# Linear attention on 32 by 32 PE tiles: block-diagonal pairs of tokens instead of groups of eight, and a block transpose for kv

## The chip, the cores and the metric

The kernel runs on one core of a Trainium2 chip (trn2). The metric is device time in microseconds (us) from start to end of one execution; the median of three runs is compared.

## What is computed

x is 8 by 512 tokens of 256 features, float32, that is 4096 tokens. Three residual parts follow each other: half of a mixture-of-experts layer (8 experts, 256 slots each), a linear-attention block with an MLP, and half of the experts layer again. The change touches the attention alone, which mixes the 16 heads of one token, never two tokens:

```python
q = (xn @ wq + bq).reshape(b, n, H, HD).transpose(0, 2, 1, 3)   # H = 16 heads of HD = 16; k and v alike
fq = jax.nn.elu(q) + 1.0
fk = jax.nn.elu(k) + 1.0
kv = jnp.einsum('bhnd,bhne->bnde', fk, v)       # per token: 16 x 16, summed over heads
qkv = jnp.einsum('bhnd,bnde->bhne', fq, kv)     # per token and head
k_sum = fk.sum(axis=1)
qk = jnp.einsum('bhnd,bnd->bhn', fq, k_sum)
attn = qkv / (qk[..., None] + 1e-06)
```

## The kernel before

The first experts stage runs to about 163 us, the middle stage (attention and MLP) to about 600 us, the second experts stage to the end. The middle stage takes 32 tiles of 128 tokens in a software pipeline: in step s of `MID_STEPS`, each engine's program does a fixed list of pieces, written out by hand, each for another tile. TensorE (PE) projects q, k and v of tile s-2 (`qkv`), forms kv of tile s-4 (`sum_kv`, L1989) and its product with the queries (`sum_att`, L2006), turns and projects the result of tile s-5 (`turn_o`, `project`), turns tile s-6 for the MLP and, from step 10, adds one group's MLP products (`up_mid`, `down_mid`). Each engine runs its list in order; semaphores join the lists. Before step 10 the PE program has no MLP work and pads itself with idle products.

The attention needs the features with heads or feature numbers on partitions. So `store_grids` (L553) writes q, k and v of a tile to HBM, and they are read back 64 bytes at a time: the tile is cut into 16 sets of eight tokens; `issue_keys` (L370) reads, for one of the eight tokens t of every set, keys onto the 16 partitions t*16 to t*16+15 and columns t*16 to t*16+15, so that `keys` [128 partitions, 16 sets, 128] is block-diagonal (the zeros were put there once by `clear_grids`, L762). `issue_queries` (L377) does the same for the queries, and one transfer brings all values (L567), with a column of ones for k_sum. With the store these are 18 transfers a tile. SyncE's queue (SP) issues them; in the first seven tiles (`HELPED`, L362) ScalarE (ACT) issues some (`help_keys`, `help_queries`, L1005 to L1019).

`sum_kv` then makes, per set, values.T @ keys: 128 partitions into 32 rows by 128 columns, four sets beside each other on the four 32-column tiles of the PE array, all into one PSUM bank (`B_ATT`). Its result is kv transposed, so it goes through ACT (`copy_kvt`, L1021, 128 by 512), four PE transposes (`turn_kv`, L2000) and a VectorE (DVE) copy (L1679) before `sum_att` multiplies it with the queries, 16 products again. `attended` (L1571) turns blocks of 32 by 32 on DVE (L1576) and divides.

Of the kernel before, what the change touches and what calls it, by code (L numbers as in the profile page):

```python
# [27 lines left out]
def build(nc, x_in, ln1_w, ln1_b, wq, bq, wk, bk, wv, bv, wo, bo, ln2_w, ln2_b,  # L28
# [19 lines left out]
    SETS = P // 8  # L48
# [10 lines left out]
    qkv_rows = nc.dram_tensor("qkv_rows", [3, T, D], F32).ap()  # L59

    with ExitStack() as ctx:
# [144 lines left out]
        with ExitStack() as phase:  # L206
            x_all = tile(phase, "x_all", [P, NT, D])
            tile(phase, "below_values", [P, 2, SETS, 32])
# [36 lines left out]
        with ExitStack() as mid:  # L245


            keys = tiles(mid, "keys_", 2, [P, SETS, P])
            queries = tiles(mid, "queries_", 2, [P, SETS, P])
            values = tiles(mid, "values_", 2, [P, SETS, 32])  # L250
            feats = tiles(mid, "feats_", 2, [P, 3 * D])
            kvt = tile(mid, "kvt_", [P, 4, P])
            kv = tile(mid, "kv_", [P, 4, P])
# [58 lines left out]
        s_st1, s_kvt, s_kvturn, s_kv = sem("kv_t_summed"), sem("kv_t_copied"), sem("kv_turned"), sem("kv_copied")  # L312
# [49 lines left out]
        HELPED = 7  # L362

        def keys_by_sp(n):
            return (4 if n == 0 else 5) if n < HELPED else 8

        def queries_by_sp(n):
            return (2 if n == 0 else 6) if n < HELPED else 8

        def issue_keys(engine, n, t):  # L370

            i, rows = n % 2, slice(n * P, (n + 1) * P)
            engine.dma_start(keys[i][t * HEADS:(t + 1) * HEADS, :, t * HD:(t + 1) * HD],  # L373
                             qkv_rows[1, rows, :].rearrange(
                                 "(s t) (h d) -> t h s d", t=8, h=HEADS)[t]).then_inc(s_kvin[i], 16)

        def issue_queries(engine, n, t):  # L377
            i, rows = n % 2, slice(n * P, (n + 1) * P)
            engine.dma_start(queries[i][t * HD:(t + 1) * HD, :, t * HEADS:(t + 1) * HEADS],
                             qkv_rows[0, rows, :].rearrange(  # L380
                                 "(s t) (d h) -> t d s h", t=8, d=HD)[t]).then_inc(s_qin[i], 16)

        def set_of(i, j):

            return 4 * j + i
# [53 lines left out]
        def _(sp):  # L439
# [113 lines left out]
            def store_grids(n):  # L553
                i, rows = n % 2, slice(n * P, (n + 1) * P)
                sp.wait_ge(s_feat, n + 1)
                sp.wait_ge(s_val, n + 1)
                sp.dma_start(qkv_rows[:, rows, :].rearrange("c p d -> p c d"),
                             feats[i][:].rearrange("p (c d) -> p c d", c=3)).then_inc(s_grid[i], 16)

            def load_keys(n):  # L560
                i, rows = n % 2, slice(n * P, (n + 1) * P)
# [5 lines left out]
                sp.dma_start(values[i][:, :, 0:HD], qkv_rows[2, rows, :].rearrange(  # L567
                    "(s t) (g e) -> (t g) s e", t=8, g=HEADS)).then_inc(s_kvin[i], 16)
                for t in range(keys_by_sp(n)):
                    issue_keys(sp, n, t)  # L570

            def load_queries(n):
                if n >= 2:
                    sp.wait_ge(s_st2, n - 1)
                for t in range(queries_by_sp(n)):
                    issue_queries(sp, n, t)
# [270 lines left out]
        def _(act):  # L847
# [146 lines left out]
            def qkv(n):  # L994
                soft = feats[n % 2][:, 0:2 * D]
                act.wait_ge(s_qk, n + 1)
                if n >= 2:
                    act.wait_ge(s_grid[n % 2], 16 * (n // 2))
# [5 lines left out]

            def help_queries(n):  # L1005
                act.wait_ge(s_grid[n % 2], 16 * (n // 2 + 1))
                if n >= 2:
                    act.wait_ge(s_st2, n - 1)
                for t in range(queries_by_sp(n), 8):
                    issue_queries(act, n, t)  # L1010

            def help_keys(n):
                act.wait_ge(s_grid[n % 2], 16 * (n // 2 + 1))
                if n == 0:
                    act.wait_ge(s_zeros, 6)
                if n >= 2:
                    act.wait_ge(s_st1, n - 1)
                for t in range(keys_by_sp(n), 8):
                    issue_keys(act, n, t)  # L1019

            def copy_kvt(n):  # L1021
                act.wait_ge(s_st1, n + 1)
                if n >= 1:
                    act.wait_ge(s_kvturn, n)
                act.copy(kvt[:], bank[B_ATT][:].rearrange("p (i c) -> p i c", i=4)).then_inc(s_kvt, 1)
# [18 lines left out]
            for s in range(MID_STEPS):  # L1044
                if at(s, 2) is not None:
                    turn_zn(s - 2)
                if s == 4:
                    help_queries(0)
                if s == 5:
                    help_keys(2)  # L1050
# [5 lines left out]
                if at(s, 4) is not None and s != 4:  # L1056
                    copy_kvt(s - 4)
# [12 lines left out]
                if 6 <= s < HELPED + 3:  # L1070
                    help_keys(s - 3)
                if at(s, 2) is not None:
                    qkv(s - 2)
                if s == 4:
                    help_keys(1)
                    copy_kvt(0)
                if routed(s, 1) is not None and routed(s, 1) < NG - 2:
                    soften(routed(s, 1))
                if s == 3:
                    help_keys(0)  # L1080
# [4 lines left out]
                if at(s, 3) is not None and 1 <= s - 3 < HELPED:  # L1085
                    help_queries(s - 3)
# [1130 lines left out]
```

## Time and profile before

| | |
|---|---|
| median of 3 runs | 728.15 us (726.8 to 728.37) |
| span of the profiled execution, first to last instruction | 726.3 us |
| PE busy | 670.9 us (92%), 6214 matmul instructions |
| DVE, ACT, POOL busy | 481.1, 420.1, 326.5 us |
| hardware DMA queue q1 (SP's) | 272298 packets, 48.9% of 16 engines' span |
| HBM traffic | 130 GB/s over the span |

The profiled execution's own time is its span and some 1.85 us around it, by the median of the runs. Busy shares are averages over stages, and matmuls overlap, so a busy PE says nothing about how well it is used. PEld is the load of the stationary operand, which is an instruction of its own. A float32 matmul of the program appears as two matmuls and two loads in the profile (called passes below); a float32r product is three matmuls of one pass each.

### The profile page before, as it was taken

To read this page: it belongs to the slowest core of one execution; us is meant where nothing else is said; L and a number is where in the kernel's file an instruction comes from. 1 tells how busy PE (TensorE), PEld (TensorE's weight loads), DVE (VectorE), ACT (ScalarE), POOL (GpSimd) and SP (SyncE) were. 2 spreads that over 40 slices of the span, in tenths; PEclk is the share of its full clock that TensorE was granted. 3 is DMA by queue.
4 is the path that set the end of the run, shared out by engine and by line. 5 is a ranking of instruction groups with operands and counts; after the bars stand their busy time and mean duration, and the time that the engine had idled before them with its cause. 6 is when DMAs were issued, how large, how long until landed. Compare 5 with 4: busy or idle time off the path is not lost.

```text
span 726.3 us, 17454 instructions
## 1 busy us (share of the span) xinstructions
PE 670.9 (92%) x6214; PEld 567.6 (78%) x6214; DVE 481.1 (66%) x1332; ACT 420.1 (58%) x841; POOL 326.5 (45%) x493
## 2 busy tenths in 40 slices
PE   7689999998777999999999999999999885999994
PEld 5449999975566788888888888888888663999994
DVE  7856757425688766767777768677676565777751
ACT  5755556502334767676767676766754642766660
POOL 5234563122232453545573664745547563353312
PEclk9879999999999999999999999999999998999998
DMA  8479788404656444544555555555433343567720
GB/s 264 149 241 322 229 270 276 139 29 119 98 99 109 91 66 90 95 87 66 101 86 85 117 84 129 68 108 91 86 73 96 116 132 109 167 215 217 219 93 29
DMA packets 287104, 95.56 MB, mean 132 GB/s; under 512 B 213989, under 2 KB 284737, under 8 KB 287019
## 3 DMA queue, kind: packets, MB, share of 16 engines
q1 hardware_dynamic: 272298, 85.48, 48.9%
q0 software_dynamic: 3840, 8.32, 3.6%
q10 hardware_dynamic: 10880, 0.66, 1.0%
q8 instruction: 50, 0.82, 0.5%
q14 instruction: 36, 0.29, 0.1%
HBM read 65.09 MB, written 29.40 MB: 130 GB/s over the span
## 4 chain that ended last, share of the span: by engine, by line
PE 75%; DVE 8%; issue 6%; ACT 4%; POOL 2%; DMA 2%; SPq 1%; ACTq 1%; POOLq 0%; DVEq 0%
PE bank L1735 68%; PE bank L1744 7%; DMA qkv_rows<-feats 1%; POOL hids L795 1%; SPq L373 1%; ACTq L373 1%; ACT hids L1038 1%; DMA x_all<-in_L_attn_q_x_dram 1%; ACT feats L1001 1%; POOL table L677 1%; ACT feats L999 0%; DVE kv_ L1679 0%; ACT ots L1063 0%; DVE sth L1687 0%; DVE att_ L1576 0%
## 5 line engine op out<-in xcount | busy, mean ns | idle before, releaser
L1735 PE MATMUL bank<-down_w,hids 128*128 128x256 f32 x768 | 105.8, 286 | 1.9 <-POOL hids L795 1.6
L1735 PE MATMUL bank<-hnts,up_w 128*128 128x512 f32 x384 | 104.4, 407 | 0.0
L795 POOL TENSOR_TENSOR hids<-hid,hids 128x512 fp32r<-128x512 f32 x64 | 83.1, 1298 | 41.0 <-ACT hids L1038 40.6
L1735 PEld LDWEIGHTS bank<-down_w,hids 128*128 128x128 f32 x768 | 95.7, 188 | 6.2 <-POOL hids L795 3.4
L1735 PE MATMUL bank<-qkv_w,xnts 128*128 128x256 f32 (+1 forms) x384 | 76.4, 346 | 5.7 <-DVE xnts L1589 4.8
L1735 PEld LDWEIGHTS bank<-hnts,up_w 128*128 128x128 f32 x384 | 67.5, 189 | 11.4
L1735 PEld LDWEIGHTS bank<-qkv_w,xnts 128*128 128x128 f32 x384 | 60.6, 189 | 18.2 <-DVE xnts L1589 7.5
L1035 ACT ACTIVATE hid<-bank,cols 128x512 f32<-128x512 f32 x64 | 44.1, 688 | 45.8 <-PE bank L1735 45.5
L786 POOL TENSOR_SCALAR sth<-sth 128x1 f32<-128x1 f32 x32 | 7.2, 226 | 125.3 <-DVE sth L1601 125.3
L1735 PE MATMUL bank<-a_w,xa_h 128*128 128x256 f32 x256 | 60.2, 379 | 0.0
L1735 PE MATMUL bank<-xa_xt,a_w 128*128 128x256 f32 x384 | 55.1, 294 | 1.4 <-DVE xa_xt L1327 1.4
L1735 PE MATMUL bank<-xb_xt,b_w 128*128 128x256 f32 x384 | 52.9, 287 | 1.4 <-DVE xb_xt L1327 1.4
L1735 PEld LDWEIGHTS bank<-xa_xt,a_w 128*128 128x128 f32 x384 | 49.0, 189 | 3.1 <-DVE xa_xt L1327 1.6
L900 ACT ACTIVATE xa_h<-bank,cols 128x256 f32<-128x256 f32 x64 | 26.8, 470 | 40.8 <-PE bank L1735 40.8
L1735 PEld LDWEIGHTS bank<-a_w,xa_h 128*128 128x128 f32 x256 | 46.3, 190 | 5.1
L1735 PEld LDWEIGHTS bank<-xb_xt,b_w 128*128 128x128 f32 x384 | 48.5, 188 | 2.4 <-DVE xb_xt L1327 1.6
L900 ACT ACTIVATE xb_h<-bank,cols 128x256 f32<-128x256 f32 x64 | 26.9, 471 | 35.0 <-PE bank L1735 35.0
L1569 DVE TENSOR_TENSOR ots<-bank,ots 128x256 fp32r<-128x256 f32 x32 | 13.5, 423 | 50.4 <-ACT ots L1063 50.4
L984 ACT CAST xnts<-bank 128x256 fp32r<-128x256 f32 x32 | 12.0, 374 | 59.9 <-PE bank L1744 57.5
L1038 ACT ACTIVATE hids<-bank,cols 128x512 fp32r<-128x512 f32 x64 | 43.6, 681 | 0.0
L1290 DVE TENSOR_TENSOR b_w<-b_raw,b_w 128x512 fp32r<-128x512 f32 x32 | 23.9, 748 | 22.4 <-ACT b_w L876 22.1
L711 POOL DMA_INDIRECT out_dram<-xb_fin,xb_slot x16 | 17.1, 1067 | 48.2 <-DVE xb_fin L1350 46.1
(272 smaller groups left out, 1546.9 us busy)
## 6 DMA issues: line engine op xcount, KB each, us to landing
qkv_rows<-feats SPq DMA_DIRECT2D x32, 384.0 KB, 3.4
a_raw<-in_L_ffn_w_dram SPq DMA_DIRECT2D x32, 256.0 KB, 4.1
a_w<-in_L_ffn_w_dram SPq DMA_DIRECT2D x32, 256.0 KB, 3.7
b_raw<-in_L_ffn_w_dram SPq DMA_DIRECT2D x32, 256.0 KB, 3.2
b_w<-in_L_ffn_w_dram SPq DMA_DIRECT2D x32, 256.0 KB, 3.0
mid_rows<-x_all SPq DMA_DIRECT2D x8, 512.0 KB, 2.9
x<-mid_rows SPq DMA_DIRECT2D x32, 128.0 KB, 2.4
values<-qkv_rows SPq DMA_DIRECT2D x32, 128.0 KB, 2.9
```

What stands on the lines that cost most here:

```text
L373: engine.dma_start(keys[i][t * HEADS:(t + 1) * HEADS, :, t * HD:(t + 1) * HD], qkv_rows[1, rows, :].rearrange("(s t) (h d) -> t h s d", t= ...
L677: pool.indirect_dma_start(table, bass.IndirectOffsetOnAxis(ap=dest_b[g % 2][:, i:i + 1], axis=0), entry_b[g % 2][:, i], None, bounds_check ...
L711: pool.indirect_dma_start(ex.target, bass.IndirectOffsetOnAxis(ap=ex.buf.slot[:, c - ex.first * ST], axis=0), ex.buf.fin[c % 4][:], None, ...
L795: pool.tensor_tensor(hids[1][u % 3][:], hid[u % 2][:], f32(hids[0][u % 3][:]), ALU.subtract).then_inc(s_hidl, 1)
L900: act.activation(ex.buf.h[u % 4][:, i], dst[:, i * CAP:(i + 1) * CAP], ACT.Relu, bias=bias).then_inc(ex.sem.relu, 1)
L984: act.copy(xnts[0][n % 2][:], bank[B_TURN][:, 0:D].rearrange("p (k t) -> p k t", k=KD)).then_inc(s_xnh, 1)
L1035: act.activation(hid[u % 2][:], bank[b][:], ACT.Gelu, bias=bias).then_inc(s_hid, 1)
L1038: act.activation(hids[0][u % 3][:], bank[b][:], ACT.Gelu, bias=bias).then_inc(s_hid, 1)
L1290: dve.tensor_tensor(low[cut], ex.raw[cut], f32(high[cut]), ALU.subtract).then_inc(ex.sem.low1, 1)
L1569: dve.tensor_tensor(ots[1][n % 2][:], bank[B_KV][:, 0:D], f32(ots[0][n % 2][:]), ALU.subtract).then_inc(s_ol, 1)
L1735: return pe.matmul(dst, left, right, start=start, stop=stop, skip_group_check=True)
L1744: return pe.matmul(dst, src, ident[:], is_transpose=True, start=start, stop=stop, skip_group_check=True)
```

## The change

The tile is cut otherwise: four bands of 32 tokens (`BANDS`), each of 16 pairs (`PAIR_TOKENS`). A pair's keys lie block-diagonally in 32 partitions (two tokens by 16 heads) by 32 columns, so `keys`, `queries`, `values` and `kv` are all [128, 16, 32], with band c on partitions 32c to 32c+31. Every product of `sum_kv` and `sum_att` is now 32 partitions by 32 by 32, on the diagonal tile (c, c) of the PE array, and there are 64 of each per tile. kv is read from PSUM by one DVE block transpose; ACT's copy, the four PE transposes and the DVE copy are gone. Two transfers each bring keys, values and queries (one per token of a pair, on every second partition), and the store is four transfers, one per band: ten in all, issued by SP alone. Two dummy tiles keep the addresses of what lies behind the now smaller ones.

```diff
-    SETS = P // 8
+    PAIR_TOKENS, BANDS = 2, 4
+    SETS = P // (PAIR_TOKENS * BANDS)
...
+    qkv_rows = nc.dram_tensor("qkv_rows", [3, T // BANDS, BANDS * D], F32).ap()
...
+        def band_rows(i, n):
+            return qkv_rows[i, n * P // BANDS:(n + 1) * P // BANDS, :]
+
+        def of_token(grid, t):
+
+            return grid[t::PAIR_TOKENS]
+
+        def store_band(engine, n, c):
+            i, q = n % 2, P // BANDS
+            engine.dma_start(qkv_rows[:, n * q:(n + 1) * q, c * D:(c + 1) * D].rearrange("i q d -> q i d"),
+                             feats[i][c * q:(c + 1) * q, :].rearrange("p (i d) -> p i d", i=3)).then_inc(s_grid[i], 16)
 
         def issue_keys(engine, n, t):
+            i = n % 2
+            engine.dma_start(of_token(keys[i], t)[:, :, t * HD:(t + 1) * HD],
+                             band_rows(1, n).rearrange("(s t) (g d) -> t g s d", t=PAIR_TOKENS, d=HD)[t]).then_inc(
+                s_kvin[i], 16)
...
             def load_keys(n):
-                sp.wait_ge(s_grid[i], 16 * (n // 2 + 1))
+                sp.wait_ge(s_grid[n % 2], 16 * BANDS * (n // 2 + 1))
...
-                for t in range(keys_by_sp(n)):
+                for t in range(PAIR_TOKENS):
                     issue_keys(sp, n, t)
+                for t in range(PAIR_TOKENS):
+                    issue_values(sp, n, t)
...
                 if n4 is not None:
-                    dve.wait_ge(s_kvturn, n4 + 1)
+                    dve.wait_ge(s_st1, n4 + 1)
                     if n4 >= 1:
                         dve.wait_ge(s_st2, n4)
-                    dve.tensor_copy(kv[:], bank[B_KV][:].rearrange("p (i c) -> p i c", i=4)).then_inc(s_kv, 1)
+                    dve.transpose(kv[:], bank[B_ATT][:].rearrange("p (s t d) -> p s d t", s=SETS, t=PAIR_TOKENS)).then_inc(s_kv, 1)
...
-                for i in range(4):
-                    for j in range(4):
-                        last = mm(bank[B_ATT][32 * j:32 * j + 32, i * P:(i + 1) * P], values[n % 2][:, set_of(i, j)],
-                                  keys[n % 2][:, set_of(i, j)], True, True)
+                for g in range(SETS):
+                    for c in range(BANDS):
+                        band = slice(32 * c, 32 * c + 32)
+                        last = mm(bank[B_ATT][band, 32 * g:32 * g + 32], values[n % 2][band, g], keys[n % 2][band, g], True, True)
                 last.then_inc(s_st1, 1)
```

`sum_att` changes as `sum_kv` does; `help_keys`, `help_queries`, `copy_kvt` and `turn_kv` are taken out with their calls.

How the instructions stand on PE in one step with the MLP, before (`hnts`, `down_w` are the MLP's, `zn_`, `on`, `kvt_`, `hn_` are operands that are turned):

```order
L1735 MATMUL bank<-hnts_0,up_w 128x512 x6
L1735 MATMUL bank<-keys,values 32x128 x16
L1744 MATMUL bank<-ident,on 128x128 x2
L1735 MATMUL bank<-qkv_w,xnts_0 128x512 x6
L1735 MATMUL bank<-qkv_w,xnts_0 128x256 x6
L1735 MATMUL bank<-down_w,hids_0 128x256 x12
L1744 MATMUL bank<-ident,kvt_ 128x128 x4
L1735 MATMUL bank<-o_w,ots_1 128x256 x6
L1744 MATMUL bank<-ident,hn_ 128x128 x2
L1735 MATMUL bank<-hnts_0,up_w 128x512 x6
L1735 MATMUL bank<-queries,kv_ 32x128 x16
```

and with the change:

```order
L1702 MATMUL bank<-hnts_0,up_w 128x512 x6
L1702 MATMUL bank<-keys,values 32x32 x64
L1711 MATMUL bank<-ident,on 128x128 x2
L1702 MATMUL bank<-qkv_w,xnts_0 128x512 x6
L1702 MATMUL bank<-qkv_w,xnts_0 128x256 x6
L1702 MATMUL bank<-down_w,hids_0 128x256 x12
L1702 MATMUL bank<-o_w,ots_1 128x256 x6
L1711 MATMUL bank<-ident,hn_ 128x128 x2
L1702 MATMUL bank<-hnts_0,up_w 128x512 x6
L1702 MATMUL bank<-queries,kv_ 32x32 x64
```

The 16 products with 128 columns become 64 with 32, twice, and the four transposes of `kvt_` between `down_w` and `o_w` are gone; nothing else on PE moves.

ACT in such a step, between the MLP's gelus and the copy of v (L1003) before:

```order
L1038 ACTIVATE hids_1<-bank,cols 128x512
L1025 COPY kvt_<-bank 128x512
L1063 CAST ots_1<-bank 128x256
L1069 ACT_TABLE_LOAD
L1069 ACTIVATE scrap<-minus_half 128x1
L999 ACTIVATE feats<-bank 128x512
L1001 ACTIVATE feats<-feats 128x512
L1003 COPY feats<-bank 128x256
```

and with the change:

```order
L1020 ACTIVATE hids_2<-bank,cols 128x512
L1039 CAST ots_0<-bank 128x256
L1045 ACT_TABLE_LOAD
L1045 ACTIVATE scrap<-minus_half 128x1
L1003 ACTIVATE feats<-bank 128x512
L1005 ACTIVATE feats<-feats 128x512
L1007 COPY feats<-bank 128x256
```

The copy to `kvt_` ahead of the cast of `ots` is gone; the rest keeps its order.

SP over one step, before:

```order
L373 DMA keys<-qkv_rows 16x16x16 x8
L549 DMA x_4<-mid_rows 128x256
L557 DMA qkv_rows<-feats 128x3x256
L379 DMA queries<-qkv_rows 16x16x16 x8
L567 DMA values<-qkv_rows 128x16x16
L373 DMA keys<-qkv_rows 16x16x16 x8
```

and with the change:

```order
L383 DMA values<-qkv_rows 64x16x16 x2
L555 DMA x_4<-mid_rows 128x256
L372 DMA qkv_rows<-feats 32x3x256 x4
L389 DMA queries<-qkv_rows 64x16x16 x2
L377 DMA keys<-qkv_rows 64x16x16 x2
L383 DMA values<-qkv_rows 64x16x16 x2
```

The store becomes four issues and the reads six, each of 1024 pieces of 64 bytes where the old ones had 256 (values 2048); their order in the step stays: store, queries, keys and values.

## Rows read from the trace of the kernel before

**Rows 1.** Busy time by stretch: us, PE, PEld, DVE, ACT, POOL, clock, DMA share, GB/s.
```profile
190.00:230.00 40.00, 31.01 (x387) 23.54 (x385) 31.42 (x76) 14.95 (x37) 12.42 (x30) 1.00 0.62 96
...
350.00:430.00 80.00, 79.79 (x881) 68.10 (x880) 59.90 (x162) 55.27 (x101) 50.02 (x82) 1.00 0.57 97
```
**Rows 2.** Timeline, PE: start, us, instruction; from `turn_o` to the transposes of one step.
```profile
247.42 0.44 PE L1744 MATMUL bank<-ident,on 128*128 128x128 f32 x2
...
251.23 0.60 PE L1744 MATMUL bank<-ident,kvt_ 128*128 128x128 f32 x4
```
**Rows 3.** One tile's rows: `keys` passes of PE: ns min/median/max, first and last start.
```profile
L1735 PE MATMUL bank<-keys,values x1024: 269/273/297, 181.7 to 541.3; 128*32 128x128 f32 x171
```
**Rows 4.** Timeline, ACT, the same stretch as rows 2.
```profile
247.68 0.59 ACT L1025 COPY kvt_<-bank 128x512 f32<-128x512 f32 x1
248.14 0.40 ACT L1063 CAST ots<-bank 128x256 fp32r<-128x256 f32 x1
...
251.11 0.35 ACT L1003 COPY feats<-bank 128x256 f32<-128x256 f32 x1
```
**Rows 5.** Timeline, loads for `o_w` behind the transposes, one step early, one late.
```profile
251.56 0.78 PEld L1735 LDWEIGHTS bank<-o_w,ots 128*128 128x128 f32 x6
...
410.82 0.35 ACT L1003 COPY feats<-bank 128x256 f32<-128x256 f32 x1
...
411.49 0.78 PEld L1735 LDWEIGHTS bank<-o_w,ots 128*128 128x128 f32 x6
```
**Rows 6.** Timeline, PE, one `sum_att`: cut at 401.71, at 401.86, and whole.
```profile
401.69 0.32 PE L1735 MATMUL bank<-queries,kv_ 128*32 128x128 f32 x4
...
401.69 0.43 PE L1735 MATMUL bank<-queries,kv_ 128*32 128x128 f32 x8
...
401.69 1.08 PE L1735 MATMUL bank<-queries,kv_ 128*32 128x128 f32 x32
```
**Rows 7.** PE on one tile: float32 passes of 256 columns, bfloat16 ones of 24.
```profile
L1735 PE MATMUL bank<-a_w,xa_h 128*128 128x256 f32 x256 | 60.2, 379 | 0.0
...
102.12 1.89 PE L1735 MATMUL bank<-a_w,xa_h 128*128 128x256 f32 x8
...
L1735 PE MATMUL bank<-rb_left_factor,rb_mark x16: 187/188/209, 604.5 to 607.9; 128*128 128x24 bf16 x16
...
604.48 0.37 PE L1735 MATMUL bank<-rb_left_factor,rb_mark 128*128 128x24 bf16 x8
```
**Rows 8.** Groups of load instructions: count, busy us, mean ns, idle before.
```profile
L1735 PEld LDWEIGHTS bank<-hnts,up_w 128*128 128x128 f32 x384 | 67.5, 189 | 11.4
...
L1735 PEld LDWEIGHTS bank<-queries,kv_ 128*32 128x32 f32 x1024 | 26.0, 109 | 11.1 <-issue 9.1 <-DVE kv_ L1679 2.0
```
**Rows 9.** Busy time of `keys` instructions, 0.1 us after a wait: PE, PEld, clock.
```profile
196.46:196.56 0.10, 0.07 (x4) 0.10 (x8) 0.00 (x0) 1.00 0.14 15
```
**Rows 10.** Timeline, ACT, early steps; last, a piece of the chain that ended last.
```profile
190.99 0.59 ACT L1025 COPY kvt_<-bank 128x512 f32<-128x512 f32 x1 [3.31 <-issue]
...
225.81 2.44 ACTq L373 DMA_DIRECT2D keys<-qkv_rows  x2
228.35 0.60 ACT L999 ACTIVATE feats<-bank 128x512 f32<-128x512 f32 x1 [2.46 <-PE bank L1735]
...
235.78 0.59 ACT kvt_ L1025
```
**Rows 11.** SP's issues: ns min/median/max; one step's keys; us from issue to landing.
```profile
L373 SPq DMA_DIRECT2D keys<-qkv_rows x234: 303/449/2612, 176.1 to 533.8; - x117
...
245.17 5.50 SPq L373 DMA_DIRECT2D keys<-qkv_rows  x8
...
qkv_rows<-feats SPq DMA_DIRECT2D x32, 384.0 KB, 3.4
```
**Rows 12.** DVE's two operations over 128x512: ns min/median/max.
```profile
L1679 DVE COPY kv_<-bank x32: 678/691/693, 185.1 to 544.9; 128x512 f32<-128x512 f32 x32
...
L1576 DVE STREAM_TRANSPOSE att_<-bank x32: 701/704/716, 187.0 to 548.3; 128x512 f32<-128x512 f32 x32
```

More of the change, by code:

```diff
@@ L245, in build @@
         with ExitStack() as mid:
-            keys = tiles(mid, "keys_", 2, [P, SETS, P])
-            queries = tiles(mid, "queries_", 2, [P, SETS, P])
+            keys = tiles(mid, "keys_", 2, [P, SETS, 32])
+            queries = tiles(mid, "queries_", 2, [P, SETS, 32])
             values = tiles(mid, "values_", 2, [P, SETS, 32])
+            tile(mid, "weights_come_early", [P, 6 * KD * D * 2])
             feats = tiles(mid, "feats_", 2, [P, 3 * D])
-            kvt = tile(mid, "kvt_", [P, 4, P])
-            kv = tile(mid, "kv_", [P, 4, P])
+            kv = tile(mid, "kv_", [P, SETS, 32])
+            tile(mid, "weights_come_early_too", [P, KD * D])
             att = tile(mid, "att_", [P, HEADS, 32])
@@ L359, in build, with issue_values @@
         LAST_SENT = PASSED_IN_STEPS - GROUP
[L362 to L368, printed above, removed]
-        def issue_keys(engine, n, t):
[L372 to L375, printed above, removed]
-        def issue_queries(engine, n, t):
[L378 to L385, printed above, removed]
+        def band_rows(i, n):
[6 more added lines that the diff above has]
+                             feats[i][c * q:(c + 1) * q, :].rearrange("p (i d) -> p i d", i=3)).then_inc(s_grid[i], 16)
+        def issue_keys(engine, n, t):
+            i = n % 2
+            engine.dma_start(of_token(keys[i], t)[:, :, t * HD:(t + 1) * HD],
+                             band_rows(1, n).rearrange("(s t) (g d) -> t g s d", t=PAIR_TOKENS, d=HD)[t]).then_inc(
+                s_kvin[i], 16)
+        def issue_values(engine, n, t):
+            i = n % 2
+            engine.dma_start(of_token(values[i], t)[:, :, 0:HD],
+                             band_rows(2, n).rearrange("(s t) (g e) -> t g s e", t=PAIR_TOKENS, e=HD)[t]).then_inc(
+                s_kvin[i], 16)
+        def issue_queries(engine, n, t):
+            i = n % 2
+            engine.dma_start(of_token(queries[i], t)[:, :, t * HEADS:(t + 1) * HEADS],
+                             band_rows(0, n).rearrange("(s t) (g h) -> t g s h", t=PAIR_TOKENS, h=HEADS)[t]).then_inc(
+                s_qin[i], 16)
         pieces = [
@@ L574, in load_queries @@
                     sp.wait_ge(s_st2, n - 1)
-                for t in range(queries_by_sp(n)):
+                for t in range(PAIR_TOKENS):
                     issue_queries(sp, n, t)
@@ L1003, in qkv @@
                 act.copy(feats[n % 2][:, 2 * D:3 * D], bank[B_V][:, 0:D]).then_inc(s_val, 1)
[L1005 to L1025, printed above, removed]
             def gelus(g, m):
@@ L1046, in _ @@
                     turn_zn(s - 2)
[L1047 to L1050, printed above, removed]
                 g_up, j_up = divmod(s - 10, GROUP)
@@ L1084, in _ @@
                     turn_h(s - 6)
-                if at(s, 3) is not None and 1 <= s - 3 < HELPED:
-                    help_queries(s - 3)
                 if 0 <= g_up < NG:
@@ L1575, in attended @@
                 dve.wait_ge(s_st2, n + 1)
-                dve.transpose(att[:], bank[B_ATT][:].rearrange("p (i t h) -> p h i t", i=4, t=8)).then_inc(s_att, 1)
+                dve.transpose(att[:], bank[B_ATT][:].rearrange("p (s t h) -> p h s t", s=SETS, t=PAIR_TOKENS)).then_inc(s_att, 1)
                 dve.wait_ge(s_att, step + 1)
@@ L2120, in _ @@
                     down_mid(g_down, 2 * j_down + 1)
-                if at(s, 4) is not None:
-                    if kv_free:
-                        pe.wait_ge(*kv_free)
-                    turn_kv(s - 4)
-                    kv_free = (s_kv, s - 3)
                 for n in turned_at(s, 0):
```

43 lines of the change are left out of this document (12 added, 31 removed).

## The prediction, made before the changed kernel was run

> **What bounds the kernel now.** I read the busy time by stretch first. From 350 to 430 us PE is busy 79.8 of 80 us at a granted clock of 1.00 (2.4 GHz), DVE 59.9, ACT 55.3 [rows 1]: with the MLP in the step nothing but PE sets the pace. From 190 to 230 us, before the MLP's products start, PE is busy 31.0 of 40 and DVE 31.4 [rows 1]; there a loop of PE, ACT and DVE sets the step. The page of the profile has SP's queue on the 16 DMA engines for half the span, but a PE that is busy all the time waits for no transfer. So the transfers, which the change is said to be about, can pay only before some 240 us; behind that the change is worth what it does to PE. `sum_kv` runs from 181.7 to 541.3 us [rows 3]; the one of tile 7 ends at 247.4 us, where `turn_o` starts [rows 2], so 25 tiles (7 to 31) stand under the PE bound, some 12.3 us each ((541.3 - 246.4)/24).
>
> **PE, what goes.** The four transposes of `kvt_`: four passes in 0.60 us, the last of which lasts 0.27 by itself, so 0.33/3 = 0.11 us apart [rows 2], 0.43 us a tile. (A pass's length is taken from its siblings of 128 columns, 273 ns [rows 3].)
>
> **PE, what is dearer.** A `sum_att` is 32 passes in 1.08 us. The timeline cut short shows how: the first four last 0.32 us together and 0.297 each, so they start some 7 ns apart, one on each 32-column tile; with the next four it is 0.43. Every 0.11 us four passes start side by side, eight times: 0.87 us [rows 3, 6]. Now there are 128 passes, 32 on each tile. What one takes is not in the trace, since no pass has 32 columns on 32 partitions; so I bound it.
> - From below: float32 passes of 256 columns start (1.89 - 0.38)/7 = 0.216 us apart [rows 7], those of 128 columns 0.109: 0.84 ns a column, so 30 ns for 32. The load of 128 columns takes 189 ns, that of 32 109 [rows 8]: 0.83 ns a column, 27 ns for 32, if the rest is a latency that overlaps. It does overlap on one tile: bfloat16 products start (0.37 - 0.19)/7 = 26 ns apart [rows 7]. And four starts 7 ns apart need 28 ns. All three give 30 ns a round, 32 x 30 = 0.96 us.
> - From above: a round costs what it costs now, 0.109 us, 32 x 0.109 = 3.5 us.
>
> I take 0.96, since it is the rows of the same kind (float32, four tiles beside each other) carried down in columns. That PE's sequencer can deliver is shown right behind a wait: within 0.1 us from 196.46 on, eight loads of `sum_kv` had started [rows 9]. In program order load and pass alternate, so the eighth load is the 15th instruction: 7 ns each at most. 256 instructions in 0.96 us want 3.8 ns each, which no row shows for so long; this is the weakest step. So +0.1 us for `sum_kv` and +0.1 for `sum_att`.
>
> Before, every product used all 128 rows of the array, and four column tiles wrote one PSUM bank side by side [rows 6]; now four row tiles write the bank `B_ATT`, each its own 32 partitions. The rule that speaks against it is in the Trainium skill, TensorEngine Tiling (Array Packing), Gotcha 1: PSUM Pressure: different row tiles cannot use one PSUM bank at the same time. No row here shows such a case; by the rule the sum would be that of the third rival below.
>
> **What stands behind the transposes.** PE's next piece, `project`, waits for ACT's copy of v. In the early step this copy ends at 251.11 + 0.35 = 251.46 us and the loads for `o_w` start at 251.56; in the late one at 411.17 and 411.49 [rows 4, 5]. So where the gap is 0.10, ACT must come earlier for PE to gain. It does: the copy to `kvt_` goes, which sits 0.46 us ahead of the cast of `ots`. But the cast waits for `turn_o`, whose end, 247.42 + 0.44 = 247.86, moves to 247.96; the cast then starts at about 248.00 in place of 248.14 [rows 2, 4], and all behind it 0.14 earlier. I count half of the gap of 0.10 as the signal's own time. So such a step gains 0.05 + 0.14 = 0.19 in its first half, and 0.09 with the 0.1 of `sum_att` off. In the late step the slack is 0.27 + 0.14, more than PE's 0.43 - 0.10 = 0.33, so it keeps 0.33, less 0.1: 0.23. I take 4 tiles of the early kind (until the turned rows of the second router come between, from step 15 on) and 21 of the late: 0.4 + 4.8 = **5.2 us less**.
>
> **DVE.** The block transpose takes the place of the copy at the same point of its list, 704 ns for 691 [rows 12]: +0.01 a tile. It now waits for `sum_kv` itself, long done. Nothing.
>
> **DMA.** SP issues 18 and a row of x now, up to 5.5 us for eight keys [rows 11]; afterwards 10, at the median 0.45 each 4.5 us. The pieces of 64 bytes are as many as before (6144 a tile). In the first steps the store's four issues push its landing 3 x 0.45 = 1.4 us back, and 3.4 us of landing are no longer covered by eight issues of queries; in return keys and values take four issues for nine, 2.3 us less, on SP alone. That is about even. ACT, however, stops helping: at 190.99 it comes to its copy after 3.31 us in which the profile shows it waiting for nothing, while its queue issued keys; at 225.81 two issues take 2.44 us, and the features start right behind them at 228.35, for which I put 0.5, an estimate; and the `kvt_` copy of 0.59 us at 235.78 is on the chain that ended last [rows 10], 0.46 in its queue. I take 1.0 + 0.5 + 0.4 = 1.9 us less. Bounds: 0 (the transfers' chain replaces it) and 4 (three issues behind one another on SP no longer stand in the way). Five steps in which the loop over DVE binds have `sum_att` in it: +0.5. Together **1.4 less**.
>
> **The sum.** 726.3 - 5.2 - 1.4 = 719.7 us of span. The median of the runs lies 1.85 us over this span: **721.5 us**. A round of 35 ns in place of 30 would add 2 x 0.16 x 30 = 10 us at most, so the forecast hangs on a few ns; with 30 ns and the DMA bounds it is 719 to 723.5, with 28 to 33 ns 717 to 728.
>
> **The rivals.**
> - **Gain eaten up.** Rounds of 32 to 34 ns, or a start that waits for four stores: 726 to 730 us; centre 728. For it: 28 ns of starts and 30 of columns leave no reserve. Chance 0.13.
> - **Load and pass take turns on a tile** (27 + 30 = 57 ns a round). `sum_kv` and `sum_att` take 1.82 us, +0.95 each. PE: 25 x (1.9 - 0.43) = +37 us, first steps +6: 771 us. It decides from about 34 ns a round on. For it: in all stages with four tiles the load ended just when the older pass had run out (109 and 109 ns), so the trace doesn't show them overlapping there; against it, one tile with 24 columns does. Chance 0.15. This is the rival on the other side.
> - **The bands take turns at the bank**, as the rule has it: 128 x 30 ns = 3.8 us, +2.97 twice; 25 x (5.9 - 0.43) = +137, first steps some +20: 885 us. For it: no row has several row tiles. Against: they write different partitions, and four column tiles share the bank now. Chance 0.08.
> - **Starts stay 26 ns apart**, as on one tile [rows 7], at either level of the clock: 128 x 26 = 3.3 us, +2.46 twice; 25 x 4.5 + 16 = +129: 857 us. Against it, four starts 7 ns apart [rows 6], but never more than four in a row. The Trainium skill, TensorE: Matmul & The Clock Gate, Part 1 ("Wait — 56ns, not 53.3ns?"), has starts never closer than about 25 ns; rows 6 speak against it where the tiles differ. Chance 0.10.
> - That the change doesn't do what it says: the program order shows 64 small products and no turn of kv, so this has none.
>
> **The numbers.** Forecast 0.54, gain eaten 0.13, turns on a tile 0.15, bank 0.08, 26 ns 0.10. About 0.2% (1.5 us) is what a measurement can tell. The forecast's own range is all but 0.02 faster; the eaten gain is same 0.06, slower 0.04, faster 0.03. Faster 0.55, same 0.08, slower 0.37. The range from 716 to 775 takes in the first three, 0.82; the likeliest alone spans 717 to 727.
>
> **What would show it.** Right: one `sum_att` of 128 passes in 1.1 to 1.2 us with its tail (0.96 + 0.27), `o_w` loads 0.05 to 0.1 us behind the copy of v, steps with MLP 0.1 to 0.25 us shorter, no ACT queue in the chain at 225 us. Wrong: passes more than 34 ns apart on a tile; `sum_kv` waiting for keys; SP's store later than the features by more than its own issue; or PE still busy all of the time at longer steps.

## The result and the profile after

| | before | after |
|---|---|---|
| median | 727.94 us (726.8 to 728.37, 4 runs) | 779.8 us (775.59 to 780.54, 4 runs) |
| ratio, 95% interval | | 1.0699 (1.067 to 1.0728) |
| span, mean granted clock | 726.3 us, 0.977 | 778.8 us, 0.953 |
| matmul instructions of PE | 6214 | 12230 |

The change makes the kernel 7% slower. The prediction said 721.5 us and a range up to 775; both are missed: it forecast a gain and there is a loss.

The page of the changed kernel: busy time, clock by slices, queues.
```profile
PE 696.0 (89%) x12230; PEld 595.8 (76%) x12230; DVE 485.8 (62%) x1332; ACT 407.8 (52%) x809; POOL 318.3 (41%) x493
...
PEclk9789999999869999999999999999999997999998
...
q1 hardware_dynamic: 279082, 86.12, 47.6%
q0 software_dynamic: 3840, 8.32, 3.3%
q8 instruction: 97, 1.59, 0.9%
```
Busy time by stretch, the same two stretches as [rows 1].
```profile
190.00:230.00 40.00, 27.52 (x975) 22.51 (x974) 22.88 (x56) 7.87 (x20) 10.02 (x25) 0.84 0.54 78
350.00:430.00 80.00, 75.58 (x1859) 65.86 (x1847) 56.83 (x163) 47.06 (x86) 38.14 (x62) 0.98 0.51 87
```
PE has twice the instructions and yet is idle for 4.4 of 80 us where it was busy for 79.8, and no other engine took over: DVE, ACT and POOL all do less in the stretch. Early on the granted clock is down to 0.84 of full speed, so a part of that stretch ran at 1.2 in place of 2.4 GHz. The queue q8, which brings PE's instructions, has 97 packets of 16 KB for 50 before: 2 x 12230 / 97, some 252 of PE's loads and passes a packet (249 before). That q8 is PE's is read from these counts, which grow together. The row of before:
```profile
q8 instruction: 50, 0.82, 0.5%
```

The timeline of PE in the changed kernel (start, us; in brackets the idle time before, and what ended it) shows the loss in both places.
```profile
207.05 1.29 PE L1702 MATMUL bank<-queries,kv_ 32*32 32x32 f32 x128
...
209.70 0.24 PE L1702 MATMUL bank<-keys,values 32*32 32x32 f32 x2
210.79 1.44 PE L1702 MATMUL bank<-keys,values 32*32 32x32 f32 x126 [0.85 <-issue]
212.16 0.33 PE L1711 MATMUL bank<-ident,on 128*128 128x128 f32 x1
214.62 0.37 PE L1711 MATMUL bank<-ident,on 128*128 128x128 f32 x1 [2.13 <-issue]
214.74 4.18 PE L1702 MATMUL bank<-qkv_w,xnts 128*128 128x512 f32 x12
...
388.00 1.05 PE L1702 MATMUL bank<-queries,kv_ 32*32 32x32 f32 x100
391.35 0.64 PE L1702 MATMUL bank<-queries,kv_ 32*32 32x32 f32 x28 [2.29 <-issue]
...
404.75 1.25 PE L1702 MATMUL bank<-queries,kv_ 32*32 32x32 f32 x116
406.58 0.36 PE L1702 MATMUL bank<-queries,kv_ 32*32 32x32 f32 x12 [0.58 <-issue]
```
An undisturbed stage of 128 passes takes 1.29 us where one of 32 took 1.08 [rows 6]: the small products do run beside each other on four row tiles. From the first load to the last that is 1.07 us, reached by 18 of the 64 stages. But many stages are broken by a pause that ends with no semaphore and no transfer of the program ("issue"), up to 2.97 us in the stage at 224.79, and between two transposes of one `turn_o` PE stands still for 2.13 us. Behind that pause `qkv` needs 4.18 us for 12 passes that take 2.35 in later steps; the mean granted clock from 212 to 219 us is 0.62. The waits of the load queue on "issue":
```profile
PEld bank L1702 <- issue: 73.9, 135, 3.5
```
Before, the same row had 35.1 us in 108 times, the longest 0.7. What lies in the pause at 389 us is shown by the DMA view of 387.3 to 390.1 us, and by the busy time from there to 391.3 (PE and PEld stand still for all of it).
```profile
q8 instruction: 1, 0.02, 6.1%
```
```profile
390.10:391.30 1.20, 0.00 (x0) 0.00 (x0) 0.00 (x0) 0.00 (x0) 1.12 (x3) 0.93 0.10 20
```
6.1% of 16 engines for 2.8 us is one DMA engine busy for 2.73 us with one packet of instructions. It ends at 390.09, and PE goes on at 391.35. Behind this pause too a part runs at the lower clock: from 392.3 to 394.3 us the granted clock is 0.50, and `down_mid` takes 2.69 us for its 12 passes in place of some 1.7. From 175 to 620 us the changed kernel has 32 pauses over 0.15 us between two products of the same stage, 31.4 us together; 21 of them, 27.9 us together, end 1.2 to 1.6 us behind the end of an instruction packet. Counting PE's loads and passes in order, these 21 pauses stand 252 to 254 instructions apart, or a whole multiple of that: always at the same place in a packet. A packet takes 0.88 to 2.73 us (median 0.96), and two never start less than 3.46 us apart. Before, no stage had such a pause.

### The profile page after: what moved, and what is told of

It is laid out like the page before. It is cut to its first block, busy times and chain, and to the rows that moved or that the text cites. A ratio compares the mean times of both kernels' runs of the same rounds, so it can differ in the third digit from the quotient of the medians.

```text
span 778.8 us, 29124 instructions
## 1 busy us (share of the span) xinstructions
PE 696.0 (89%) x12230; PEld 595.8 (76%) x12230; DVE 485.8 (62%) x1332; ACT 407.8 (52%) x809; POOL 318.3 (41%) x493
## 4 chain that ended last, share of the span: by engine, by line
PE 77%; issue 8%; DVE 5%; POOL 3%; ACT 2%; DMA 2%; SPq 1%; POOLq 0%; DVEq 0%; ACTq 0%
PE bank L1702 71%; PE bank L1711 6%; POOL hids L799 1%; DMA values<-qkv_rows 1%; DMA qkv_rows<-feats 1%; ACT feats L1005 1%; DMA x_all<-in_L_attn_q_x_dram 1%; ACT feats L1003 1%; POOL table L681 0%; SPq L377 0%; DVE ra_mark L1445 0%; SPq L372 0%; DVE att_ L1543 0%; DVE kv_ L1646 0%; DMA x<-mid_rows 0%
## 5 line engine op out<-in xcount | busy, mean ns | idle before, releaser
L1702 PE MATMUL bank<-down_w,hids 128*128 128x256 f32 x768 | 108.8, 291 | 4.8 <-POOL hids L799 3.6
L1702 PEld LDWEIGHTS bank<-down_w,hids 128*128 128x128 f32 x768 | 98.2, 193 | 7.9 <-issue 3.7
L1702 PE MATMUL bank<-qkv_w,xnts 128*128 128x256 f32 (+1 forms) x384 | 83.2, 368 | 1.3 <-DVE xnts L1556 1.3
L1702 PEld LDWEIGHTS bank<-qkv_w,xnts 128*128 128x128 f32 x384 | 66.3, 205 | 16.2 <-DVE xnts L1556 2.8
L1702 PEld LDWEIGHTS bank<-keys,values 32*32 32x32 f32 x4096 | 41.3, 105 | 31.2 <-issue 29.3
L1702 PE MATMUL bank<-keys,values 32*32 32x32 f32 x4096 | 46.6, 195 | 18.7 <-issue 16.2
L1702 PEld LDWEIGHTS bank<-queries,kv_ 32*32 32x32 f32 x4096 | 41.9, 105 | 24.5 <-issue 22.6
L1702 PE MATMUL bank<-queries,kv_ 32*32 32x32 f32 x4096 | 47.2, 195 | 12.5 <-issue 9.0
```

Of the source, the lines that this page charges most:

```text
L1702: return pe.matmul(dst, left, right, start=start, stop=stop, skip_group_check=True)
```

## The experiments

Three theories. **Supply:** PE's instructions come in packets, each good for some 252 loads and passes, and a run of 256 small ones uses a packet up faster than the next can be had. **Array:** small products, or four row tiles on one bank, cost more than thought. **Transfers:** ten larger ones, four stores, no help by ACT.

The table is added up from the starts of PE's loads and passes in each trace, in us a step between the first load of `sum_kv` of tile 7 and that of tile 31, over 24. "Stages" runs from the first load of `sum_kv` and `sum_att` to the start of the next product, "pauses" are those over 0.15 us inside them. "Lead" is the time from the first `sum_kv` to that of tile 7. These columns come from the one execution that was traced, which can lie off the median: e1's took 788.0 us, e11's 755.4. Each ratio is to executions of the kernel before of the same session, with medians of 728.5 to 729.3 us for e1 to e12.

| kernel | us (median) | ratio (95%) | step | stages | pauses | packets of q8 | lead |
|---|---|---|---|---|---|---|---|
| before | 727.9 | | 12.25 | 2.04 | 0 | 1.08 | 64.7 |
| after | 779.8 | 1.070 | 13.66 | 3.46 | 0.86 | 2.54 | 81.1 |
| e1 before, split | 792.4 | 1.088 (1.085 to 1.091) | 14.06 | 3.57 | 1.00 | 2.58 | 78.6 |
| e2 half | 711.0 | 0.975 (0.972 to 0.978) | 11.45 | 1.44 | 0.02 | 1.58 | 65.8 |
| e3 in 4 parts | 777.4 | 1.066 (1.062 to 1.069) | 13.50 | 3.09 | 0.31 | 2.58 | 80.7 |
| e4 few, ten transfers | 701.8 | 0.962 (0.961 to 0.964) | 11.02 | 0.43 | 0 | 0.71 | 66.9 |
| e5 block only, stride 2 | 747.9 | 1.025 (1.022 to 1.028) | 12.93 | 2.08 | 0.04 | 1.04 | 66.4 |
| e6 16 columns | 787.5 | 1.083 (1.080 to 1.085) | 13.98 | 3.44 | 0.99 | 2.54 | 80.1 |
| e7 few, stride 2 | 742.4 | 1.019 (1.017 to 1.020) | 12.59 | 0.73 | 0.01 | 0.62 | 68.6 |
| e8 in 8 parts | 788.1 | 1.082 (1.081 to 1.084) | 14.01 | 3.11 | 0 | 2.58 | 81.6 |
| e9 block only | 717.3 | 0.985 (0.983 to 0.987) | 11.87 | 2.04 | 0 | 1.04 | 62.3 |
| e10 and ACT helps | 717.2 | 0.985 (0.982 to 0.988) | 11.87 | 2.04 | 0 | 1.04 | 63.0 |
| e11 small kv only | 748.6 | 1.026 (1.022 to 1.029) | 12.59 | 2.42 | 0.13 | 1.79 | 77.9 |
| e12 few, 18 transfers | 711.5 | 0.976 (0.973 to 0.979) | 11.63 | 0.73 | 0.01 | 0.62 | 64.4 |

**e1. Only more instructions.** The kernel before, each product cut in four; the edit is the same in `sum_att`.
```
 for i in range(4):
-    for j in range(4):
-        mm(bank[B_ATT][32 * j:32 * j + 32, i * P:(i + 1) * P], values[:, set], keys[:, set])
+    for m in range(4):
+        for j in range(4):
+            c0 = i * P + 32 * m
+            mm(bank[B_ATT][32 * j:32 * j + 32, c0:c0 + 32], values[:, set], keys[:, set, 32 * m:32 * m + 32])
```


> The kernel before with each attention product of 128 columns cut into four of 32 columns: same operands, same 18 transfers, same transposes of kvt_, all 128 rows of the array; sum_kv and sum_att have 128 passes each as in the changed kernel. Supply theory (PE is held up because its instructions arrive too slowly when 256 of them want to run in about 1.1 us): the stalls without a releaser come here too, some 40 us or more of them, time 765 to 790 us. Array theory (passes of 32 rows on four row tiles are what costs): no stalls, 726 to 735 us. Transfer theory (the ten larger transfers cost): 726 to 735 us.

792.4 us. With the transfers, the operands, all 128 rows and the transposes of before, the count of instructions alone makes the loss, and the same pauses come:
```profile
200.90 1.61 PE L1735 MATMUL bank<-keys,values 128*32 128x32 f32 x104 [2.04 <-issue]
...
211.00 0.26 PE L1735 MATMUL bank<-queries,kv_ 128*32 128x32 f32 x5 [2.08 <-issue]
...
216.12 0.32 PE L1735 MATMUL bank<-keys,values 128*32 128x32 f32 x12 [2.50 <-issue]
```
In 24 of 30 pauses PE goes on 1.2 to 1.6 us behind a packet's end. Between these 24 too lie 251.5 to 254 loads and passes, or a multiple. Four row tiles and the ten transfers are cleared of the bulk of the loss. The time lies 2 us above what the supply theory gave.

**e2. Half of the passes.** `for g in range(0, SETS, 2)` in both stages; the attention of half of the tokens is left out.

> The changed kernel with every second set left out of sum_kv and sum_att (64 passes each; half of the tokens' attention is not computed), transfers as in the changed kernel. Supply theory: the stalls shrink by far more than half of the passes' own time: array -0.53 us for each of 50 stages under the PE bound (-27 us), stalls -30 us or more: 715 to 725 us. Array theory (each pass costs more than it should, everywhere): half of all the loss, 750 us. Transfer theory: only the array's own -27 us: 750 us.

711.0 us, 69 below the changed kernel, for 0.53 us less array time in each of 64 stages, which is 34. A stage has 128 instructions now, half a packet, and the pauses are gone. The ten transfers are all still there. The time is 4 us below the 715 to 725 that I gave.

**e3. The same passes in two parts a stage**, in the steps with MLP: half of `sum_kv` behind `qkv`, half of `sum_att` inside `up_mid`.
```
-                    sum_kv(s - 4)
+                    sum_kv(s - 4, 0, 8)
...
                     qkv(s - 2, v_free)
+                    sum_kv(s - 4, 8, 16)
```


> The changed kernel; in the steps with MLP sum_kv and sum_att are each cut into two parts of 64 passes with qkv and half of an up_mid between them. No pass is added or left out, but four changes between small and large products come on top in a step. Supply theory: half a page of small products behind seconds of large ones is supplied in time, most of the stalls in the steps with MLP go: -20 to -35 us, 745 to 760 us. Array theory: the same passes, plus 4 changes of 0.1 us in 26 steps: +5 to +10 us, 785 us. Transfer theory: 780 to 785 us.

777.4 us: a miss for both. The pauses fall from 0.86 to 0.31 us a step, as the supply theory wants, but the step gains only 0.16: two more entries into small products cost what the pauses gave back. I had priced the entries at 0.1 and thought half a packet safe anywhere. It isn't, if the next 128 follow within 2 us, as the halves of `sum_att` do around one half of `up_mid`: packets came no closer than 3.5 us in this run.

**e4. Next to no attention on PE.** One set of 16 is left in both stages; the rest of the attention is left out.

> The changed kernel with only one set of four passes left in sum_kv and in sum_att (the rest of the attention is not computed), transfers all as in the changed kernel. Array time left out: about 1.2 us for each of 50 stages, 60 us. Supply theory: the stalls go too, so 50 us or more below what that makes of 779.8: 665 to 680 us, unless DVE then sets the pace. Transfer theory: 720 us and stalls or waits still there. Array theory (the 32x32 passes are the whole of the loss and have no stalls outside): 665 to 680 us as well.

701.8 us, above what I gave. The step stops at 11.02: in the stretch from 350 to 430 us DVE is busy for 72.1 of 80, and PE waits for it in places.
```profile
350.00:430.00 80.00, 76.13 (x606) 63.56 (x604) 72.09 (x191) 58.23 (x108) 52.77 (x81) 1.00 0.65 111
```
So the run doesn't tell the theories apart by its time. What it does show is that with ten transfers and no ACT help the lead is 66.9 us for 64.7 before, and for 64.4 in e12, which has as little attention on PE and the 18 transfers: at the start the transfers cost some 2 us, not 16.

**e5 and e7. The other half of the change by itself.** I put the transpose of blocks into the kernel before and left its 32 passes a stage. The blocks then hold two tokens of each band of 32, so queries are loaded to fit, and `turn_o` writes its columns in token order. e7 is e5 with only 2 of the 16 products of a stage. (The code is written short.)
```
-                turn_kv(s - 4)
-                dve.tensor_copy(kv[:], bank[B_KV])
+                dve.transpose(kv[:], bank[B_ATT][:].rearrange("p (s t d) -> p s d t", s=SETS, t=2))
...
-            dma_start(queries[t * 16:(t + 1) * 16, :, t * 16:(t + 1) * 16], rows 8 s + t)
+            dma_start(queries[32 * c + u:32 * c + 32:2, :, t * 16:(t + 1) * 16], rows 32 c + 2 g + u)
...
-                    turn(bank[B_KV][:, k * P:(k + 1) * P], on[:, k * P:(k + 1) * P])
+                    turn(bank[B_KV][:, k * P:(k + 1) * P].rearrange("p (c g u) -> p g c u", c=4, u=2), on[...])
```


> The kernel before with one part of the change alone: kv comes by the transpose of blocks on VectorE (no copy to kvt_, no four transposes on PE, no ACT copy). The passes stay at 32 of 128 columns a stage, the transfers at 18 a tile; queries of two tokens per band are loaded so that the blocks fit, and turn_o writes its columns in the order of the tokens. The sum's term for what goes is tested by itself: PE -0.43 us a step under the PE bound (0.2 where ACT is near), 6 to 10 us less over 25 tiles, and 0 to 4 less at the start: 715 to 723 us beside 728. If instead something else takes up the 0.43 (ACT's copy of v, DVE), 725 to 730. No stalls inside sum_kv and sum_att by the supply theory, since each has 64 instructions.

> The kernel of the run e5_block_only with only two of its 16 products left in sum_kv and sum_att (the rest of the attention is not computed): next to no attention on PE, like e4_few (701.8 us), but with the 18 transfers and ACT's help. The difference of the two is that of the transfers alone. Supply theory: 697 to 706 us. Transfer theory (the ten larger ones cost by themselves): below 690 us.

747.9 and 742.4 us: both miss, and nearly without attention on PE it is as slow. No pause of the kind above lies in the stages (the 0.04 of the table are six rounds of 0.17 to 0.19 us in one stage at 367 us, where the granted clock is 0.51); PE waits for queries (12.6 us) and keys (7.5 us). It does so late: the first steps with MLP take 11.63 us, later ones up to 17.0. The rows of SP's issues of queries (ns min/median/max), before and in e5, and the one that waited in e5:
```profile
L379 SPq DMA_DIRECT2D queries<-qkv_rows x238: 303/452/3035, 179.2 to 538.3; - x119
```
```profile
L381 SPq DMA_DIRECT2D queries<-qkv_rows x238: 561/609/2090, 179.9 to 563.0; - x119
...
  PE bank L1728: 12.6, 8
```
Written to every second partition, each issue takes SP 0.16 us longer at the median, and SP is nearly full already: before, one step's issues are
```profile
400.02 0.50 SPq L549 DMA_DIRECT2D x<-mid_rows  x1
400.62 0.90 SPq L557 DMA_DIRECT2D qkv_rows<-feats  x1
401.56 4.13 SPq L379 DMA_DIRECT2D queries<-qkv_rows  x8
405.79 0.40 SPq L567 DMA_DIRECT2D values<-qkv_rows  x1
406.23 5.60 SPq L373 DMA_DIRECT2D keys<-qkv_rows  x8
411.87 0.45 SPq L549 DMA_DIRECT2D x<-mid_rows  x1
```
11.53 us of issues (0.50 + 0.90 + 4.13 + 0.40 + 5.60) in a step of 11.85. With 8 x 0.16 = 1.3 us more a step SP falls behind. SP stood right behind PE as the next limit, which I had not seen.

**e9 and e12. The same with neighbouring partitions.** e12 is e9 with 2 of the 16 products of a stage. (The code is written short, against e5.)
```
-            queries[32 * c + u:32 * c + 32:2, :, ...]
+            queries[t * HD:(t + 1) * HD, :, ...]
...
-                dve.transpose(kv[:], bank[B_ATT][:].rearrange("p (s t d) -> p s d t", s=SETS, t=2))
+                dve.transpose(kv[:], bank[B_ATT][:].rearrange("p (s c) -> p s c", s=SETS))
```


> As e5_block_only (747.9 us), but the rows of a block of kv stay in the order (token, dimension), so that a transfer of queries writes 16 neighbouring partitions as before; in e5_block_only every second one, and an issue took SP 0.76 us in place of 0.52. If SP's issues (13 us of a step of 12.9) set the step there: back to 11.6 us of issues, less than PE's 12.25 - 0.43 = 11.8, 715 to 724 us. If turn_o's column order or the transpose of blocks is what costs: it stays at 740 to 750.

> As e9_block_rows with two of 16 products left in sum_kv and sum_att (the rest of the attention is not computed), 18 transfers. Beside e4_few (701.8 us, ten transfers), nearly the same PE work: if the 18 issues of SP are a limit of their own the step can't be below some 11.6 us, 712 to 722 us. Transfer theory (the ten larger ones are dearer): below 695 us.

717.3 us for e9: faster than both kernels, by 1.5% beside the one before (0.9825 to 0.9874). A tile's `sum_kv` starts 11.63 us behind the last one, in steps like these, where it took 11.94 before:
```profile
267.34 1.08 PE L1728 MATMUL bank<-keys,values 128*32 128x128 f32 x32
...
278.97 1.08 PE L1728 MATMUL bank<-keys,values 128*32 128x128 f32 x32
...
290.60 1.08 PE L1728 MATMUL bank<-keys,values 128*32 128x128 f32 x32
```
```profile
270.31 1.08 PE L1735 MATMUL bank<-keys,values 128*32 128x128 f32 x32
...
282.25 1.08 PE L1735 MATMUL bank<-keys,values 128*32 128x128 f32 x32
```
(The second pair is of before.) e12, nearly without attention on PE, takes 711.5 us, just under the 712 to 722 that I gave, and PE waits for keys in it, from 350 to 520 us:
```profile
PE bank L1728 <- DMA keys<-qkv_rows: 11.0, 10, 4.6
```
In e4, with ten transfers, PE waits for no keys in that stretch and once for values, 1.1 us, and its step is 0.61 us shorter. So ten transfers are worth something late in the kernel, but only once PE has dropped below some 11.6 us a step, and in the full kernels PE never did. The 11.6 is a mean and no fixed floor: steps of e12 take from 10.65 us in the first half to 15.83 late, so SP keeps up for a while with the 18 issues and then falls behind.

**e10. Is SP the limit of e9?** One issue of keys and one of queries of every later tile go to ACT.

> As e9_block_rows, with one transfer of keys and one of queries of every later tile issued by ACT too (SP issues 16 in place of 18). If SP is still the next limit in e9_block_rows: 2 to 6 us less than it. If PE sets the step: the same within 1 us, or 1 to 4 us more where ACT comes later to the copy of v.

717.2 us, the same step of 11.87. PE sets the pace of e9.

**e6. What sets the rate of small products?** Same instructions, 16 columns on both sides; three quarters of each block are left out.
```
-    mm(bank[B_ATT][band, 32 * g:32 * g + 32], values[band, g], keys[band, g])
+    mm(bank[B_ATT][32 * c:32 * c + 16, 32 * g:32 * g + 16], values[band, g, 0:16], keys[band, g, 0:16])
```


> The changed kernel with 16 columns in place of 32 on both sides of every product of sum_kv and sum_att (three quarters of each block are not computed): the number of instructions is the same, their columns halve. Instruction theory (about 4.6 ns for each load and pass, whatever its size): a round of four passes stays at 37 ns, the stalls stay, 770 to 782 us. Array theory (columns set the round): a round of 18 to 20 ns, a stage under the PE bound 0.55 us shorter, 750 us, and still stalls.

787.5 us. An undisturbed stage:
```profile
397.64 1.22 PE L1702 MATMUL bank<-keys,values 32*16 32x16 f32 x128
```
1.22 us for 1.29 with twice the columns. From the first load to the last it is 1.02 for 1.07: 1.02/127 = 8.0 ns a pass, 4.0 for each load or pass. Half of the columns save 5% of the time, so the instructions set the rate, not the columns. The two kernels have the same instructions in the same order, and 20 of e6's pauses behind a packet come at the very same instruction, counted from the start, as 20 of the 21 of the changed kernel: the place in the packets makes a pause, not the work. The total came out 5 us above the bound I gave; the mean clock is 0.935 for 0.953, which fits, though I have not separated it.

**e8. The sharper form of the supply theory.** Four parts a stage, between the products of `up_mid`, `qkv` and `down_mid`.
```
+                if between is not None:
+                    sum_att(between, 0, 4)
                 for k in range(KD):
                     product(bank[b][:], ...up_w...)
+                    if k == 0 and between is not None:
+                        sum_att(between, 4, 8)
```


> The changed kernel; in the steps with MLP sum_kv and sum_att are cut into four parts of 16 products each, laid between the products of up_mid, qkv and down_mid. Supply theory in its sharper form (256 instructions of PE can't be had in less than some 3.5 us, wherever they stand): with 128 instructions in a row nowhere left and large products between all parts, the gaps over 0.15 us inside the stages, 0.86 us a step in the changed kernel and 0.31 in e3_spread, fall below 0.1. Each of the six further entries to small products costs 0.2 to 0.25 us, so the time doesn't fall: 775 to 800 us. Array theory: gaps as many as in the changed kernel.

788.1 us, and not one pause left in these steps. The timeline:
```profile
395.44 0.45 PE L1702 MATMUL bank<-queries,kv_ 32*32 32x32 f32 x32
395.82 0.96 PE L1702 MATMUL bank<-hnts,up_w 128*128 128x512 f32 x3
396.71 0.45 PE L1702 MATMUL bank<-queries,kv_ 32*32 32x32 f32 x32
397.09 0.96 PE L1702 MATMUL bank<-hnts,up_w 128*128 128x512 f32 x3
```
The same 128 passes a stage, 2.58 packets a step for 2.54, no pause: it isn't the products, it is how closely 256 instructions follow each other. (The five pauses that are left in the kernel, before the steps with MLP, stand at the same five instructions as in the changed one.) The pauses don't come for free, though. A step without them should take 11.87 + 2 x 0.20 = 12.27 us (e9 and two small stages, see e11); it takes 14.01, so each of the six further entries costs 0.29, if all of the difference is theirs.

**e11. One small stage a step.** `sum_kv` on 32 by 32 tiles as in the changed kernel, `sum_att` with 16 products of 128 columns and eight transfers of queries.
```
-                for g in range(SETS):
-                    for c in range(BANDS):
-                        mm(bank[B_ATT][band, 32 * g:32 * g + 32], kv[band, g], queries[band, g])
+                for i in range(4):
+                    for j in range(4):
+                        mm(bank[B_ATT][32 * j:32 * j + 32, i * P:(i + 1) * P], kv[:, 4 * j + i], queries[:, 4 * j + i])
```


> The changed kernel with 32 by 32 tiles in sum_kv alone; sum_att has 16 products of 128 columns as before (eight transfers of queries). 256 instructions in one run in a step in place of twice 256. Supply theory: the gaps inside the stages fall to less than a third (below 0.25 us a step, 0.86 in the changed kernel), a step of 12.0 to 12.4 us: 722 to 738 us. Array theory (each stage costs half of the loss): 750 us.

748.6 us, above both what I gave and e9. The pauses are down to 0.13 us a step, below the 0.25 that I gave. A part of the rest is transfers: here PE waits 11.9 us for queries and 6.2 for values over the kernel. The lead is 77.9 us; what makes it so long with one small stage was not tried. The traced execution was also the slowest of five (755.4 us), so the step of 12.59 is a high one. Where nothing is disturbed, the starts give the price of one small stage by itself:
```profile
272.68 1.28 PE L1704 MATMUL bank<-keys,values 32*32 32x32 f32 x128
...
284.51 1.29 PE L1704 MATMUL bank<-keys,values 32*32 32x32 f32 x128
...
296.34 1.20 PE L1704 MATMUL bank<-keys,values 32*32 32x32 f32 x118
298.15 0.28 PE L1704 MATMUL bank<-keys,values 32*32 32x32 f32 x10 [0.60 <-issue]
```
11.83 us a step for 11.63 in e9: +0.20.

## Why the prediction was wrong

The change put the span up by 52.5 us: 24 x 1.405 = 33.7 in the steps from tile 7 to 31, 16.4 in the lead, and some 2.3 before and behind.

- **"PE, what goes", -0.43 us a step: right.** It stood in e9 by itself: the steps went from 12.25 to 11.87 on average, -0.38, and the time by 11 us. The sum without its two terms for dearer products (5.2 + 25 x 0.2, and 1.9 at the start) gives 12. The slack in front of ACT's copy of v was there: from 250 to 530 us of e9 PE waits for no copy of v.
- **DVE's transpose, +0.01 a tile: right.** 706 ns at the median against 704 [rows 12].
- **"PE, what is dearer", +0.1 us a stage: wrong in size.** A round of four passes takes 4 x 1.07/127 = 34 ns in place of 30, and a stage costs +0.20 by e11. Columns and loads had given 27 to 30 ns; e6 shows that neither sets it. With this term right, the sum is 12.27 us a step, the same as before, or the rival "gain eaten up", 728 us. The bank, the 26 ns and the turns on a tile were wrong: all three need more than 1.07 us for a stage. (The 26 ns of [rows 7] were read at 604 us, where the granted clock is 0.50, and set beside rows at 1.00.) So the Trainium skill's rule in TensorEngine Tiling (Array Packing), Gotcha 1: PSUM Pressure, does not show here: four row tiles wrote one bank, a round of four starting every 34 ns.
- **"256 instructions in 0.96 us": the step that failed.** I called it the weakest and asked only for the rate of one instruction after another, shown for 15 of them right behind a wait [rows 9]. That rate holds within a packet. I did not ask where the next packet comes from. The page of before had the row: q8 with 50 packets, 0.82 MB. One packet is worth some 250 of PE's instructions, so a stage uses up a whole packet in a little over one microsecond, twice a step, where packets start 3.46 us apart at the closest; no term and no rival priced that. The pauses are 0.86 us a step inside the stages. With the short ones and the entries (0.16), longer `down_mid` behind them (3.17 us a step for 2.92 in e9) and 0.11 in the rest, the step is 1.39 above 12.27; that is 33 of the 52.5 us. The Trainium skill, Runtime: NRT & Kernel Launch, Instruction fetch mechanics, calls crossing a 16 KiB boundary "mostly hidden". That holds for the kernel before, where packets never started less than 7 us apart; in the changed one it does not.
- **Start and transfers, -1.4 us: wrong, it was +16.4.** The loss here is not of transfers either: the lead is 66.9 us with ten transfers and no passes, 65.8 with half of the passes, 78.6 with 18 transfers and 128 passes a stage. In this stretch the changed kernel has six pauses inside stages, 9.3 us together, and the one of 2.1 us in `turn_o`; the other 5 us were not taken apart. PE's granted clock fell too (0.84 over the 40 us, 1.00 before), and `qkv` takes 4.18 us for 2.35. The lower clock mostly stands behind pauses in the trace, but it is also 0.58 from 187.3 to 190.2 us, before the first one at 198.9; in e4, with few passes, it is low too (0.78 from 200 to 240 us, where PE is busy for 26.9 of 40 us), so a low clock there needs no pauses, only a PE that is idle for other reasons. One term was read too low besides: the changed kernel's issues of keys, queries and values hold SP for 0.67 us each at the median, not the 0.45 of the old ones.
- **"A PE that is busy all the time waits for no transfer": right for the kernel before, but too short.** SP had 0.3 us to spare in the step shown. That was not priced, and e5 fell over it.
- **The chances.** Of the 0.37 for slower, 0.33 lay on mechanisms that the runs refute, so that the range, which ended at 775 us, came within 5 us of the result is luck: its upper part stood for load and pass taking turns on a tile.

## What to carry to other kernels

Count PE's instructions, loads and passes both, before cutting products into smaller tiles, and hold the count against the row of the instruction queue: here a packet of some 250 came every 3.5 us at the closest, so a burst of 256 small ones can stall although the array has room for it. A change with two halves is worth trying in halves: the transpose of blocks alone gives 1.5%, and with the small tiles the kernel is 7% slower. And beside the engine that binds, add up the issues of the DMA queue in one step; it may be the next limit, a few tenths of a microsecond away.

## What the runs showed of the hardware that I had not expected

- Small products on four tiles start one load or pass every 4.0 to 4.2 ns, whether they have 16 or 32 columns (1.02 and 1.07 us from first to last load of 128), 32 rows or 128 (the stages of e1 undisturbed take 1.30 us).
- In 21 of 32 pauses (24 of 30 in e1) PE goes on 1.2 to 1.6 us behind the end of an instruction packet, and a packet itself takes 0.88 us to 2.73 us. What makes one long was not tried.
- A DMA to every second of 32 partitions, with the same count of pieces, takes SP 609 ns to issue in place of 450 at the median (e5, e9).
- The pauses sit at fixed places of the instruction stream, a multiple of some 252 loads and passes apart, and come back at the same instructions in other kernels as far as the list is the same (e6, e8).
- An entry from large products into small ones and back costs at most about 0.29 us, an estimate from e8's step against e9's and e11's.
